# A fourth relation by Strassen's seven products, and key-row requests that wait one group further back, in a graph and feed-forward kernel

## Chip, cores and metric

The kernel runs on one core of one Trainium2 chip. The metric is the device time in microseconds (us) of one execution; for several executions their median is given.

## The reference, cut to what matters

Four layers follow one another on a node matrix x of 625 rows and 1024 columns, all float32. The change touches the first of them, a relational graph layer, and the list of edges that the third one uses too:

```python
xn = layernorm(x)
out = xn @ root + bias
for r in range(8):                                   # eight relations
    mask = (edge_type == r)
    sums = segment_sum(xn[src] * mask[:, None], dst, 625)
    mean = sums / maximum(segment_sum(mask, dst, 625), 1.0)[:, None]
    out = out + mean @ weight[r]                     # weight[r] is 1024 x 1024
```

There are 20,625 edges. After this come a gate, an 8-bit dense layer, a graph convolution over the same edges and a mixture of experts; the change leaves all of them as they are.

## The kernel before, in words

**Order of the mathematics.** The kernel computes h = xn @ weight[r] first for every relation (nine "units": relations 1 to 8, then unit 0, which is the root matrix), stores each h to memory, and then multiplies it by the relation's 625 x 625 matrix of edge counts ("spread"). `UNITS` gives the order 1, 2, ..., 8, 0; the index `n` in the loops is the place in that order.

**Products.** The 625 rows are five chunks of 125 (`C = 5`). A weight matrix is 16 tiles of 128 x 512: eight steps k over its rows, two halves `hf` of its columns. Every float32 number is kept as a high and a low part, and `three` (line 581) issues three matmuls for a chunk and a tile. `by_tile` (line 584) does one half of a unit: it takes five of the eight PSUM banks, one for each chunk, and runs 8 steps x 5 chunks x 3 = 120 matmuls, so a plain unit is 240. Five banks in turn out of eight mean that a new half finds three banks free; for its fourth and fifth chunk it waits until the first two chunks of the half before have been evicted. In unit 0 VectorE evicts; in plain units 1 to 8 ScalarE does, in `h_copy` (line 1104), one copy and one store for each of the five chunks, after it has done step k = 7 of that half.

**Units by Strassen's scheme.** The units in `FAST` (before: 6, 7, 8) go through `fast_unit` (line 637). The first four chunks are two 2 x 2 block problems, each done with seven block products instead of eight; the fifth chunk is computed plainly. That is 28 tiles (the seven `KINDS` times four), 72 products, 216 matmuls. Three of the seven weight blocks are loaded and used as they are; the other four are sums that VectorE makes in `fast_after` (line 1458, eight additions of 128 x 1024 by line 1418). VectorE also combines products (lines 1430, 1438, 1446), and ScalarE makes three copies of products (lines 1114, 1119) and three of the ten evictions; VectorE makes the other seven. The stationary sides, sums of blocks of xn, are made once, by `s_made` (VectorE, line 1496, 20 operations of line 1494 and 8 of line 1489) and `s_high` (ScalarE, line 1144, 8 casts), in the steps with odd k of the unit with n = `S_AT`: n = 3 (unit 4) before. ScalarE waits in `s_high` until VectorE has made the sum.

**The tile ring.** Weight tiles come over the SP queue (line 467) in groups of four into stages: two buffers in turn for plain units, and three further ones (C, D, E) for Strassen units. ScalarE makes the high part (line 403) and VectorE then the low part (line 412) in a ring of ten slots (`RT = 10`). At step k both do the tile nine places ahead; ScalarE can write a slot only when TensorE has used the tile ten places back.

**Key windows.** The counts of edges are built from a list of keys, one for each edge. VectorE compares 41 groups of four columns of keys with broadcast key rows (`key_window`, line 1564: four operations of line 1574, then two small ones, lines 1578 and 1581). `WINDOWS` says at which steps k of a plain half a window lies (before: 0, 2, 4, 6 of every half, from the second half of unit 1 on, with one window in the first half), and `KEYS_IN_FAST` at which tiles of a Strassen unit (before: 3, 10, 17, 24). By that the 41 windows are over within unit 6. The key rows lie in four buffers. ScalarE requests them by `key_rows` (line 1174), which first waits for the comparison that used the buffer four groups back; `next_key_rows` (line 1208) is called at the place of each window. At the place of window w, ScalarE's own counter g is w - 1, and before the change it requests group g + 5 = w + 4: it waits there for window w itself.

**From the windows to the spread.** GpSimd adds the counts of each group by four indirect DMAs (line 2215) into one of two scratch matrices. Up to group 9 all go to one of them, and each group waits until the group before has landed; from group 10 on they alternate. The scratch matrices are zeroed by DMAs, those of the second one on the SP queue, two with each of the weight groups 8 to 15. When the last group has landed and the last Strassen unit is evicted (`h_made` on VectorE, `if i - F0[u] == 37`), GpSimd fetches the matrices of relations 0 and 1 (lines 2243 and 2220), ScalarE copies them (`adjacency_copy`, line 1178), and TensorE begins to spread. The SP queue loads the h of each relation into the same two stages.

```python
            def key_rows(g):
                on.wait_ge(*at("equal", g - 4))
                e.dma_start(KR[:, g % 4, :], keyflat[...]...)
```

## Time and profile before

| what | value |
|---|---|
| median of 3 runs | 1142.88 us (1140.48 to 1143.81) |
| the profiled execution | 1138.64 us, of which the span is 1136.9 us |
| TensorE busy (matmul) | 1077.9 us, 95% of the span, 5433 matmuls |
| TensorE busy (weight load) | 902.2 us, 79% |
| VectorE busy | 751.3 us, 66% |
| ScalarE busy | 406.3 us, 36% |
| GpSimd busy | 400.9 us, 35% |
| mean granted TensorE clock | 0.976 of full speed |
| DMA | 217.34 MB, 191 GB/s over the span |

In the profile PE is TensorE (PEld its weight loads), DVE is VectorE, ACT ScalarE, POOL GpSimd, SP the queue of SyncE. A row names line, engine, operation, and the tiles written and read. The busy time of an engine is the union of its instructions. In a timeline each row begins with its start and its duration in us, and in brackets stands how long the engine was idle before it and who ended the wait. In a table by windows each engine has its busy time and the number of its instructions in that stretch; PEclk is the granted TensorE clock, where 1.00 is 2.4 GHz and 0.50 is 1.2 GHz. Matmuls overlap, so a matmul's own duration (0.40 us for 512 columns) is longer than the distance between two of them.

### The profile page before, as it was taken

Reading aid. Unit: us, or ns where it says so; the run is one execution under the profiler, and the core shown is the slowest. Engines: PE = TensorE matmul, PEld = TensorE weight load, DVE = VectorE, ACT = ScalarE, POOL = GpSimd, SP = SyncE. Lnnn points to the kernel's source line nnn. Section 1 sums busy time; section 2 is a strip of 40 time slices with the busy share of each in tenths; the row PEclk is TensorE's granted clock in tenths of the full one; section 3 lists DMA queues with packets and bytes.
Section 4 is the critical chain, followed back from the end, with each engine's and each line's share of the span. In section 5 each row is a group of like instructions: output and inputs, shape, how many; then the busy total and the mean of one; then the engine's idle time right before and its main releaser. Section 6 shows DMA issues by size and latency. Waiting matters only on the chain.

```text
span 1136.9 us, 14471 instructions
## 1 busy us (share of the span) xinstructions
PE 1077.9 (95%) x5433; PEld 902.2 (79%) x5433; DVE 751.3 (66%) x1529; ACT 406.3 (36%) x631; POOL 400.9 (35%) x272
## 2 busy tenths in 40 slices
PE   6979999897999999999999999799979999999996
PEld 5868888675888888888999999788856878878874
DVE  7466666767679785325666677466378738866657
ACT  3323222222243434312323333261433514337752
POOL 6044444688788888113322340000020000311016
PEclk9989999998999999999999999999989999989998
DMA  9988999777948465897999933442242011588757
GB/s 331 403 264 243 277 275 277 163 165 193 286 74 233 102 157 122 189 249 193 267 243 238 257 100 111 146 178 93 75 86 81 25 70 37 190 259 294 267 181 254
DMA packets 94474, 217.34 MB, mean 191 GB/s; under 512 B 29978, under 2 KB 46173, under 8 KB 85947
## 3 DMA queue, kind: packets, MB, share of 16 engines
q1 hardware_dynamic: 39488, 137.19, 36.6%
q0 software_dynamic: 37504, 48.18, 21.0%
q10 hardware_dynamic: 17406, 30.97, 9.3%
q8 instruction: 46, 0.75, 0.3%
q14 instruction: 30, 0.25, 0.1%
HBM read 149.59 MB, written 66.71 MB: 190 GB/s over the span
## 4 chain that ended last, share of the span: by engine, by line
PE 85%; DVE 10%; ACT 2%; issue 1%; DMA 1%; ACTq 0%; POOLq 0%; DVEq 0%; SPq 0%
PE ps L581 68%; PE ps L889 5%; PE ps L926 4%; DVE EQ L1574 3%; DVE rl L412 2%; PE ps L853 2%; PE ps L571 1%; ACT rh L403 1%; PE ps L904 1%; DVE V L1494 1%; PE ps L937 1%; PE ps L1020 1%; PE ps L806 1%; ACT He L1104 1%; PE ps L870 1%
## 5 line engine op out<-in xcount | busy, mean ns | idle before, releaser
L412 DVE TENSOR_TENSOR rl<-stage,rh 128x512 fp32r<-128x512 f32 (+1 forms) x276 | 222.7, 830 | 228.0 <-ACT rh L403 224.1
L403 ACT CAST rh<-stage 128x512 fp32r<-128x512 f32 (+1 forms) x276 | 188.5, 709 | 434.7 <-PE ps L581 237.6
L2215 POOL DMA_INDIRECT adj_scratch<-cnt,idx x164 | 271.4, 1655 | 157.6 <-issue 53.5
L581 PE MATMUL ps<-rh,xTh 128*125 128x512 f32 x680 | 271.5, 399 | 21.5 <-ACT He L1104 20.7
L581 PE MATMUL ps<-rl,xTh 128*125 128x512 f32 x680 | 269.3, 396 | 0.0
L581 PE MATMUL ps<-rh,xTl 128*125 128x512 f32 x680 | 269.1, 396 | 0.0
L581 PE MATMUL ps<-rh,Ar 125*125 125x342 f32 x600 | 190.1, 322 | 0.8 <-DVE U L1669 0.8
L581 PE MATMUL ps<-rl,Ar 125*125 125x342 f32 x600 | 189.5, 321 | 0.0
L581 PEld LDWEIGHTS ps<-rh,xTh 128*125 128x125 f32 x680 | 127.3, 187 | 54.8 <-ACT He L1104 22.1
L581 PEld LDWEIGHTS ps<-rh,xTl 128*125 128x125 f32 x680 | 127.4, 187 | 31.8
L581 PEld LDWEIGHTS ps<-rl,xTh 128*125 128x125 f32 x680 | 127.7, 188 | 30.7
L1574 DVE SCALAR_TENSOR_TENSOR EQ<-KR,kc,later 128x512 bf16<-128x512 f32 x164 | 113.4, 748 | 0.0
L581 PEld LDWEIGHTS ps<-rh,Ar 125*125 125x125 f32 x600 | 112.4, 187 | 1.1 <-issue 1.0
L581 PEld LDWEIGHTS ps<-rl,Ar 125*125 125x125 f32 x600 | 112.5, 188 | 0.0
L1669 DVE SCALAR_TENSOR_TENSOR U<-ps,rc,U 125x342 f32<-125x342 f32 (+1 forms) x120 | 66.2, 569 | 26.9 <-PE ps L581 24.6
L2233 POOL TENSOR_TENSOR Atot<-Atot,Ar 128x3125 f32<-128x3125 f32 x7 | 44.4, 6347 | 69.8 <-ACT Ar L1186 69.8
L581 PE MATMUL ps<-rh,uTh 128*125 128x512 f32 x160 | 63.5, 397 | 0.0
L2265 POOL DMA_DIRECT2D X<-in_fbias x6 | 6.0, 1118 | 162.2 <-ACT U L1157 162.2
L581 PE MATMUL ps<-rl,uTh 128*125 128x512 f32 x160 | 63.1, 394 | 0.0
L581 PE MATMUL ps<-rh,uTl 128*125 128x512 f32 x160 | 63.1, 394 | 0.0
L581 PE MATMUL ps<-rh,Sx 128*125 128x512 f32 x120 | 45.3, 394 | 0.0
L1104 ACT COPY He<-ps 125x512 f32<-125x512 f32 x59 | 34.1, 586 | 20.2 <-ACT He L1104 14.8
(295 smaller groups left out, 1494.0 us busy)
## 6 DMA issues: line engine op xcount, KB each, us to landing
stage<-in_w_rel SPq DMA_DIRECT2D x26, 1024.0 KB, 6.6
stage<-h_scratch SPq DMA_DIRECT2D x24, 855.0 KB, 7.1
stage<-in_w_e SPq DMA_DIRECT2D x16, 1024.0 KB, 5.2
adj_scratch<-Z POOLq DMA_DIRECT2D x16, 767.0 KB, 19.7
adj_scratch<-Z SPq DMA_DIRECT2D x16, 767.0 KB, 10.1
h_scratch<-He ACTq DMA_DIRECT2D x40, 257.0 KB, 9.2
h_scratch<-He ACTq DMA_DIRECT2D x40, 256.0 KB, 4.0
KR<-key_scratch ACTq DMA_DIRECT2D x37, 256.0 KB, 6.2
```

Of the source, the lines that this page charges most:

```text
L403: e.copy(h, s).then_inc(*a_hi.up(*[("hi", t) for t in step(i)]))
L412: e.tensor_tensor(l, s, h.bitcast(F32), ALU.subtract).then_inc(*v_lo.up(*[("lo", t) for t in step(i)]))
L571: ins = e.transpose(ps[:, b, j * P:(j + 1) * P], source[:, c, k * 128:(k + 1) * 128], ident[0:P, 0:P])
L581: ins = e.matmul(ps[0:P, b, 0:width], a, m, start=first and n == 0, stop=last and n == len(parts) - 1, skip_group_check=again)
L853: ins = e.matmul(ps[0:P, b, :], AT[:, k, c * P:(c + 1) * P], m[:, k, HALF[hf]], start=k == 0 and m is gh, stop=k == C - 1 and m is gl)
L889: ins = e.matmul(ps[:, b, 0:vn], a[:, ws], m[:, k, v0:v0 + vn], start=k == 0 and j == 0, stop=k == 7 and j == 2)
L926: ins = e.matmul(ps[0:HC, b, :], a, m, start=k == 0 and q == 0, stop=k == 1 and q == 2)
L1104: e.copy(He[0:P, n % NHE, 2:514], ps[0:P, b, :]).then_inc(*a_out.up(("he", u, c, hf)))
L1574: e.scalar_tensor_tensor(out=EQ[:, j, :], in0=KR[:, g % 4, :], scalar=kc[:, t:t + 1], in1=later[:, j0:j0 + TG * 128], op0=ALU.is_equal, op ...
L1669: e.scalar_tensor_tensor(out=U[:, c, to], in0=ps[0:P, b, cols], scalar=rc[:, r, c:c + 1], in1=U[:, c, to], op0=ALU.mult, op1=ALU.add).then ...
L2215: e.indirect_dma_start(accd[to], bass.IndirectOffsetOnAxis(ap=idx[:, n:n + 1], axis=0), cnt[:, n:n + 1], None, compute_op=ALU.add).then_in ...
L2233: e.tensor_tensor(flat, flat, arf, ALU.add).then_inc(*p_row.up(("total", r)))
```

## The change

Relation 5 becomes a Strassen unit as well (`FAST = (5, 6, 7, 8)`). The stationary sums move one unit earlier (`S_AT = 2`, unit 3). The 41 windows are laid out anew: five in unit 1 as before, eleven in unit 2, eight in unit 3, eleven in unit 4, six in unit 5, none after it. At the place of window w ScalarE now requests group g + 4 = w + 3, so that it waits for window w - 1. The third load of the root matrix goes into stage D, so the two common stages alternate the other way round from there on; ScalarE's copy of relation 1's matrix, which overwrites that stage, waits for the low parts of those four tiles. The last three evictions of the last Strassen unit lie one tile earlier on VectorE.

```diff
--- before.py
+++ after.py
@@ -39,7 +39,8 @@
 SW = 2048
 NHE = 8
 NB = 8
-WINDOWS = {(n, hf): (0, 2, 4, 6) for n in range(R + 1) for hf in range(2)}
+WINDOWS = {(0, 1): (0, 2, 4, 6), (1, 0): (0, 1, 2, 4, 5, 6), (1, 1): (0, 1, 3, 5, 6), (2, 0): (0, 2, 4, 6), (2, 1): (0, 2, 4, 6),
+           (3, 0): (0, 1, 2, 4, 5, 6), (3, 1): (0, 1, 3, 5, 6), (8, 0): (), (8, 1): ()}
 SOLE = 10
 ROWS = [[(slice(0, 128), c * P, 128)] for c in range(C - 1)] + [[(slice(0, 112), 500, 112), (slice(112, P), 612, 13)]]
 HALF = (slice(0, 512), slice(512, D))
@@ -47,11 +48,11 @@
 LATE = [(R - 2, 0), (R - 1, 0), (R - 2, 1), (R - 2, 2), (R - 1, 1), (R - 1, 2)]
 ORDER = [(r, q) for r in range(R - 2) for q in range(3)] + LATE
 UNITS = [*range(1, R + 1), 0]
-FAST = (6, 7, 8)
+FAST = (5, 6, 7, 8)
 KINDS = ("b11", "t2", "t3", "t1", "t4", "b21", "b22")
 FL = 4 * len(KINDS)
-KEYS_IN_FAST = (3, 10, 17, 24)
-S_AT = 3
+KEYS_IN_FAST = {5: (2, 7, 12, 17, 22, 26)}
+S_AT = 2
 
 
 class Count:
@@ -351,7 +352,8 @@
             else:
                 for q in range(4):
                     kind = ("root",) if u == 0 else ("rel", u - 1)
-                    group(w_root[q] if u == 0 else w_rel[4 * (u - 1) + q], 128, *[(*kind, q // 2, q % 2 * 4 + t) for t in range(4)])
+                    group(w_root[q] if u == 0 else w_rel[4 * (u - 1) + q], 128, *[(*kind, q // 2, q % 2 * 4 + t) for t in range(4)],
+                          where=3 if (u, q) == (0, 2) else None)
         h_of = lambda r: hd[r].rearrange("p (c w) -> p c w", c=C)
         for r, q in ORDER:
             group(h_of(r)[:, :, q * TH:(q + 1) * TH], P, *[("h", r, q, k) for k in range(C)], width=TH)
@@ -1180,6 +1182,9 @@
                 if r == 0:
                     on.wait_ge(*at("slot zero"))
                     on.wait_ge(*at("fast", FAST[-1], "b22", ("E", 2)))
+                if r == 1:
+                    for k in range(4):
+                        on.wait_ge(*at("lo", tile["root", 1, k]))
                 if r >= 2:
                     on.wait_ge(*at("spread", r - 2, 2, C - 1))
                     on.wait_ge(*at("total", r - 2))
@@ -1206,18 +1211,15 @@
             g = 0
 
             def next_key_rows(g):
-                if g < NG - 1:
-                    if g == 0:
-                        key_rows(4)
-                    if g + 5 < NG:
-                        key_rows(g + 5)
+                if g + 4 < NG:
+                    key_rows(g + 4)
                 return g + 1
 
             for n, unit in enumerate(UNITS):
                 if unit in FAST:
                     for l in range(FL):
                         highs(F0[unit] + l + RT)
-                        if l in KEYS_IN_FAST:
+                        if l in KEYS_IN_FAST.get(unit, ()):
                             g = next_key_rows(g)
                     continue
                 for hf in range(2):
@@ -1450,7 +1452,7 @@
                     if i - F0[u] == 29:
                         for p in range(2):
                             h_made(u, 2 * p + 1, 0, banks.of["fast", u, "Y", p], V2[0:P, p, :], ALU.add, ("fast", u, "t4", ("Y", p)), ("v2", u, p))
-                    if i - F0[u] == 37:
+                    if i - F0[u] == (36 if u == FAST[-1] else 37):
                         for p in range(2):
                             h_made(u, 2 * p, 1, banks.of["fast", u, "Z", p], V2[0:P, p, :], ALU.subtract, ("fast", u, "b22", ("Z", p)), ("v2", u, p))
                         h_made(u, 4, 1, banks.of["fast", u, "E", 2], V5[0:P, :], ALU.subtract, ("fast", u, "b22", ("E", 2)), ("v5", u))
@@ -1629,7 +1631,7 @@
                 if unit in FAST:
                     for l in range(FL):
                         lows(F0[unit] + l + RT)
-                        if l in KEYS_IN_FAST and g < NG:
+                        if l in KEYS_IN_FAST.get(unit, ()):
                             key_window(g)
                             g += 1
                     continue
```

## Rows read from the trace of the kernel before

**Rows 1.** Section 1 of the page: TensorE's busy time.

```profile
PE 1077.9 (95%) x5433; PEld 902.2 (79%) x5433; DVE 751.3 (66%) x1529; ACT 406.3 (36%) x631; POOL 400.9 (35%) x272
```

**Rows 2.** What TensorE waited for, 0 to 520 us: total, times, longest.

```profile
PE ps L581 <- ACT He L1104: 20.7, 3, 8.2
```

**Rows 3.** Table by windows: start and end, busy us and instructions of each engine.

```profile
50.00:100.00 50.00, 43.55 (x183) 34.62 (x182) 30.54 (x83) 10.91 (x19) 19.20 (x12) 0.93 0.81 255
150.00:200.00 50.00, 50.00 (x218) 40.19 (x217) 30.65 (x84) 13.97 (x24) 25.67 (x16) 1.00 1.00 288
200.00:250.00 50.00, 43.95 (x184) 34.94 (x183) 35.24 (x82) 13.35 (x23) 37.43 (x23) 0.93 0.72 165
250.00:300.00 50.00, 41.79 (x174) 33.11 (x174) 33.81 (x83) 14.11 (x25) 40.81 (x26) 0.93 0.83 210
```

**Rows 4.** Groups of instructions, 0 to 500 us: busy, mean ns, idle before.

```profile
L403 ACT CAST rh<-stage 128x512 fp32r<-128x512 f32 x132 | 78.6, 620 | 214.8 <-DVE idx L1581 127.5 <-PE ps L581 55.5 <-DMA stage<-in_w_rel 11.7
L412 DVE TENSOR_TENSOR rl<-stage,rh 128x512 fp32r<-128x512 f32 x132 | 88.2, 691 | 128.8 <-ACT rh L403 128.8
L1574 DVE SCALAR_TENSOR_TENSOR EQ<-KR,kc,later 128x512 bf16<-128x512 f32 x164 | 113.4, 748 | 0.0
L1418 DVE TENSOR_TENSOR stage<-stage,stageC 128x1024 f32<-128x1024 f32 x6 | 7.3, 1219 | 0.0
```

**Rows 5.** Timeline of TensorE: first matmul after each of the three waits.

```profile
81.88 0.79 PE L581 MATMUL ps<-rh,xTh 128*125 128x512 f32 x1 [6.45 <-ACT He L1104]
...
228.28 0.79 PE L581 MATMUL ps<-rh,xTh 128*125 128x512 f32 x1 [6.05 <-ACT He L1104]
...
266.11 0.79 PE L581 MATMUL ps<-rh,xTh 128*125 128x512 f32 x1 [8.21 <-ACT He L1104]
```

**Rows 6.** Timeline: one place in units two halves apart, and in two Strassen units.

```profile
135.04 0.58 ACT L1104 COPY He<-ps 125x512 f32<-125x512 f32 x1
...
190.50 0.58 ACT L1104 COPY He<-ps 125x512 f32<-125x512 f32 x1
...
398.40 0.68 DVE L1430 TENSOR_TENSOR He<-ps,V 125x512 f32<-125x512 f32 x1
...
448.49 0.68 DVE L1430 TENSOR_TENSOR He<-ps,V 125x512 f32<-125x512 f32 x1
```

**Rows 7.** Timeline of ScalarE and VectorE in unit 4, which makes the sums.

```profile
195.64 0.62 ACT L403 CAST rh<-stage 128x512 fp32r<-128x512 f32 x1 [0.40 <-ACT He L1104]
...
200.08 0.62 ACT L403 CAST rh<-stage 128x512 fp32r<-128x512 f32 x1 [3.82 <-DVE idx L1581]
...
200.73 0.69 DVE L412 TENSOR_TENSOR rl<-stage,rh 128x512 fp32r<-128x512 f32 x1 [0.66 <-ACT rh L403]
...
227.65 0.58 ACT L1104 COPY He<-ps 125x512 f32<-125x512 f32 x1
...
232.78 0.62 ACT L403 CAST rh<-stage 128x512 fp32r<-128x512 f32 x1 [0.40 <-ACT He L1104]
...
265.47 0.58 ACT L1104 COPY He<-ps 125x512 f32<-125x512 f32 x1
```

**Rows 8.** The indirect adds of GpSimd (line 2215), all 164: shape and landing.

```profile
L2215 POOL DMA_INDIRECT adj_scratch<-cnt,idx x164: 1531/1543/2568, 67.8 to 455.1; - x164
...
DMA to landing us min/median/max: 2.9/4.9/14.4
```

**Rows 9.** Timeline from the free-running adds to the first spread.

```profile
205.87 1.54 POOL L2215 DMA_INDIRECT adj_scratch<-cnt,idx  x1 [9.40 <-DMA adj_scratch<-cnt,idx]
...
455.09 1.54 POOL L2215 DMA_INDIRECT adj_scratch<-cnt,idx  x1 [0.30 <-issue]
...
476.32 0.95 POOL L2243 DMA_DIRECT2D AT<-adj_scratch  x1 [19.69 <-DVE rl L412]
...
511.29 2.81 ACT L1186 CAST Ar<-AT 128x3125 fp32r<-128x3125 f32 x1
...
526.80 0.32 PE L581 MATMUL ps<-rh,Ar 125*125 125x342 f32 x1
```

## The prediction

> **What bounds the kernel now.** The page first: TensorE is busy 95% of the span [rows 1], so a matmul less is time less, if nothing else takes its place. The view of waits for the first 520 us comes next: TensorE lost 20.7 us in three waits, all for ScalarE's evictions of products (line 1104), and next to nothing for weights [rows 2]. The table by windows prices them whole: an undisturbed stretch of 50 us has 218 matmuls, 0.2294 us each; the three stretches with a wait have 183, 184 and 174. That is 35, 34 and 44 matmuls short: 8.0, 7.8 and 10.1 us, 25.9 in all. It is more than the waits themselves (6.45, 6.05 and 8.21 us [rows 5]) because the granted clock is 0.93 in each of these stretches against 1.00 in the undisturbed one [rows 3]: after each wait TensorE restarts at the lower level, 1.2 GHz, and a restart costs some 1.8 us.
>
> Why is the eviction late? The view of groups says that ScalarE's casts of weights stood idle 127.5 us for VectorE's `idx`, the end of a key window, while VectorE's low parts stood idle 128.8 us for ScalarE's casts [rows 4]. The two engines run in lock-step: ScalarE stops at each request for key rows until the window of the same place is over. TensorE notices only where both are behind: at the end of unit 1, whose weights come late, and at the end of both halves of unit 4, where VectorE has the stationary sums too.
>
> **Part 1: a fourth relation.** Two evictions that lie two plain halves apart are 190.50 - 135.04 = 55.46 us apart; the same combination in two successive Strassen units is 448.49 - 398.40 = 50.09 us apart [rows 6]. 24 matmuls of 0.2294 us would be 5.5; I take the measured difference, **5.4 us** less.
>
> What it adds lies beside this: 12 more casts on ScalarE (0.62 each, 7.4 us), against seven evictions fewer and three copies more; on VectorE 12 more low parts (0.69, 8.3 us), eight sums (1.22, 9.8 us) and eleven combinations (0.68, 7.5 us) [rows 4, 6]. One window is four comparisons of 0.68 (113.4 us over 164, with their overlap) and two small ones, about 3.1 us. VectorE in unit 5 is then 28 low parts (19.3), sums (9.8), combinations (7.5) and six windows (18.6): 55.2 us against TensorE's 50.1, too much by 5.1 us (less where instructions overlap). The cover is the ring: VectorE works nine tiles ahead, at 50.1 / 28 = 1.8 us a tile some 16 us, and unit 6, with no windows, has 36.6 us of work in 50.1 and pays back. In unit 4's second half, where unit 5's eight sums are made already, it is eight low parts, eight sums and five windows: 5.5 + 9.8 + 15.5 = 30.8 against 27.7, late by 3.1 more. Together 8.2 us, half of the cover: nothing for TensorE. If the cover were gone, these 8 us would be the price.
>
> **Part 2: requests one group back.** ScalarE at window w waits for w - 1, one step or more past. Where windows lie two steps apart it was over long ago; where they lie at adjacent steps, one step of TensorE is 15 x 0.2294 = 3.44 us and VectorE needs 3.1 + 0.6, so ScalarE waits some tenths. The buffers get their rows three windows ahead instead of four: at least three steps, 10 us.
>
> *End of unit 1.* Without the stops ScalarE is at the eviction when TensorE has the product. Its last cast there needs weights whose load follows VectorE's low parts; VectorE was in those parts in time for TensorE, so I take the whole **8.0 us**; from below 0, if the load holds it.
>
> *The unit with the sums* (4 before, 3 after; with the same windows at the same steps, and 28 operations of VectorE and 8 casts in either place). Here ScalarE stays tied to VectorE: at each odd step it waits in `s_high` for the sum. So only part goes. The chain before: first eviction 190.50, first cast of the half 195.64, next first eviction 227.65, cast 232.78, eviction 265.47 [rows 6, 7]: evictions 5.1 us a half, work 32.0 and 32.7, or 37.2 and 37.8 where TensorE needs 27.7. The change takes from each window what VectorE loses when its low part has to wait for a cast held up by the request: 0.66 us [rows 7], some 0.7 with the gaps; four a half, 2.8 us. ScalarE also comes to the unit about 0.9 us sooner. First wait: 6.05 - 2.8 - 0.9 = 2.3 us. Second: the chain is 5.1 + 29.9 = 35.0 against 27.7, so 7.3 us and a restart of 1.8. Sum 11.4 in place of 7.8 + 10.1 = 17.9: **6.5 us** less. Bounds: 0 (ScalarE's order sets the pace all the same) and 17.9 (VectorE catches up). Between them the row of the 0.66 us is nearest.
>
> *Eleven windows in units 2 and 4.* Halves with six windows ask VectorE for 5.5 + 18.6 = 24.1 us, with five 21.0, in 27.7: fits.
>
> **Edits with one answer.** Root load in stage D and the wait for its four low parts, alternation of stages, one eviction group a tile earlier: no price. A root tile is split nine tiles before its use, and `adjacency_copy(1)`, behind which ScalarE's casts of h are queued, comes after all root tiles. The loads, stores, zero DMAs of SP and the 37 requests are the same in number; SP's stay tied to their group numbers. The latter have as cover the matmuls; if a load came late, I would see ScalarE wait for `stage`.
>
> **What is late next.** GpSimd's adds run without pause from 205.87 to 456.6 and don't depend on the windows any more by then; the fetch at 476.32 waited 19.69 us for VectorE's last evictions [rows 9]. With TensorE 19.9 us earlier that point is 456.4, and the fetch is set by the adds: 456.6 + 4.9 of landing [rows 8] = 461.5. From fetch to the end of ScalarE's copy it took 511.29 + 2.81 - 476.32 = 37.8 us, part of it waiting for its turn: 499.3. The first spread matmul, 526.80 before, is due at 506.9. So 7.6 us of cover are left of 12.7.
>
> **The sum.** 5.4 + 8.0 + 6.5 = 19.9 us. Against the profiled execution: 1138.6 - 19.9 = 1118.7. That execution lies 4.2 us below the median of the runs; against the median, 1142.9 - 19.9 = **1123.0 us**.
>
> **The rivals.**
> *A. As above*, 1123; its own range 1118 to 1128. Chance 0.55.
> *B. All three waits go.* For it: VectorE has 34 to 35 us of work in the 50 of the two stretches [rows 3], so it isn't full, and ScalarE is freed of 127.5 us of idling. Against it: `s_high` still ties them. 1142.9 - 5.4 - 25.9 = 1111.6. Chance 0.14.
> *C. VectorE takes over as the bound* where windows are packed, above all in units 4 and 5: its 8.2 us are not covered because it comes late out of the unit with the sums. 1123.0 + 8.2 = 1131.2, about 1127 if half shows. Chance 0.17.
> *D. The request's wait doesn't go*, since window w - 1 is unfinished too (at adjacent steps it is so by tenths, by the figures above): only 5.4 stays, 1137.5. Chance 0.05.
> *E. GpSimd is held up by VectorE.* An add took 1.54 us at the median but up to 2.57 [rows 8], and from 205.87 to 455.09 the 123 distances average 2.03 us against 1.84 (1.54 and the 0.30 of issue) [rows 9]: 23 us lost, in a stretch where VectorE's operations mostly read two tensors in SBUF. The change puts 20 more such operations into unit 5. If the loss doubled, the adds would end at 479.6, the matrix be ready at 479.6 + 4.9 + 37.8 = 522.3, and TensorE wait 15.4 us: 1138.4. Chance 0.05: 20 operations more don't double it. The Trainium skill ("SBUF — State Buffer", section "SBUF: two separate sides") speaks against the change in this way: VectorE with two SBUF inputs and GpSimd share a port pair as an exclusive lock, and a DMA whose descriptors GpSimd makes can starve behind it. By that rule E, by the median row A; the trace agrees with it only as far as the 2.57 goes.
> *F. Slower than before: the first ten groups of adds.* They run one after another, each waiting for the landing of the last, 67.8 to 205.87 [rows 8, 9], 13.8 us a group, at a DMA share of 1.00 [rows 3]. The change packs more requests and the zero DMAs of SP into that stretch. It decides once the fetch passes 506.9 - 37.8 = 469.1; to be 0.3% slower than before, the spread must begin after 530.2, the fetch after 492.4, which is 31 us past 461.5, or 3.1 us more for each of the ten groups. 3.5 us each give 1147. Against it: 37 requests stay 37, and the longest landing of any add is 14.4 us. Chance 0.04.
>
> **How the numbers follow.** A measurement of this kernel can tell about 0.3%, 3.4 us, from no change. A, B, C, D, E are faster by more than that: 0.96, less 0.02 for what D and E hold near the edge; F is slower, 0.04; within 0.3% 0.02. The range reaches from B, 1111, to C, 1131: it leaves out D, E and F (0.14) and a little at the ends.
>
> **What would show it.** Right: a Strassen unit of 50.1 us as the fifth unit; no wait near 75 us; ScalarE's idling for `idx` from 127.5 to under 20 us; TensorE's waits for evictions near 10 us in two, in unit 3 (about 160 and 195 us); the fetch of line 2243 released by an add and not by VectorE; the first spread near 507. Wrong: no wait at all in unit 3 (B), a wait of TensorE for `rl` in units 4 to 6 (C), ScalarE idle for `idx` as before (D), TensorE idle before the first spread (E, F).

## The result, and the profile after

| | before | after |
|---|---|---|
| median of 4 runs | 1142.82 us (1140.48 to 1143.81) | 1157.99 us (1157.09 to 1160.41) |
| the profiled execution; its span | 1138.64 us; 1136.9 us | 1158.23 us; 1156.5 us |
| mean granted TensorE clock | 0.976 | 0.965 |

The kernel became slower: ratio 1.0148, 95% interval 1.0123 to 1.0172. The forecast was 1123.0 us, with a range from 1111 to 1131 us.

The code has moved by two lines (581 is now 583, 412 is 414). The first section of the page after the change, to set beside [rows 1]:

```profile
PE 1077.9 (93%) x5409; PEld 900.9 (78%) x5409; DVE 777.8 (67%) x1560; ACT 411.8 (36%) x639; POOL 407.1 (35%) x272
```

24 matmuls fewer are there, but the busy time is the same: some of it was run at the lower clock. Section 2, 40 slices of 28.9 us each, shows where:

```profile
PE   6999998999999999953999999899978999999995
...
PEclk9999999999999999986899999999998999989997
```

TensorE's 18th and 19th slices (491 to 549 us) stand at 5 and 3, and the clock falls to 8, 6 and 8 from the 18th to the 20th. What TensorE waited for after the change, whole span, the four largest:

```profile
PE ps L583 <- issue: 25.7, 1, 25.7
PE ps L573 <- DVE U L1548: 9.2, 1, 9.2
PE ps L583 <- DVE rl L414: 8.9, 1, 8.9
PE ps L583 <- ACT He L1106: 7.0, 2, 4.9
```

The last row answers to [rows 2]: 20.7 us in three waits became 7.0 in two. The first and third are new. (`rl` is the low part of a tile, `Ar` a relation's matrix, `He` the evicted product.) TensorE's timeline says where each one ends (the 9.2 us of line 573 lies at the very start of the kernel, where it was 9.6 us before the change):

```profile
161.01 0.49 PE L583 MATMUL ps<-rh,xTh 128*125 128x512 f32 x1 [2.08 <-ACT He L1106]
...
195.71 0.58 PE L583 MATMUL ps<-rh,xTh 128*125 128x512 f32 x1 [4.87 <-ACT He L1106]
...
532.53 0.62 PE L583 MATMUL ps<-rh,Ar 125*125 125x342 f32 x1 [25.74 <-issue]
...
551.64 0.65 PE L583 MATMUL ps<-rh,Ar 125*125 125x342 f32 x1 [8.87 <-DVE rl L414]
```

**The account.** The row at 532.53 is the first spread matmul. TensorE was free for it at 532.53 - 25.74 = 506.79 us. Before the change it began at 526.80 [rows 9], without a wait. So up to there the change had saved **20.0 us**, and the forecast had said 19.9. Then it gave back 25.7 and 8.9. The span grew by 19.6, so 19.6 + 20.0 - 25.7 - 8.9 = 5.0 us remain. No row shows them one by one, but the table by windows shows the lower clock level around both waits:

```profile
500.00:550.00 50.00, 17.03 (x80) 15.09 (x78) 10.55 (x6) 8.74 (x4) 15.01 (x7) 0.70 0.78 191
510.00:532.00 22.00, 0.00 (x0) 0.00 (x0) 0.00 (x0) 2.36 (x1) 4.97 (x4) 0.50 0.95 247
552.00:560.00 8.00, 8.00 (x36) 8.00 (x36) 7.05 (x17) 0.00 (x0) 0.00 (x0) 0.64 0.93 275
```

In an idle stretch the granted clock is 0.50 (1.2 GHz), and just after the second wait it is still 0.64. After that nothing differs: from ScalarE's copy of relation 2's matrix (552.29 us before, 572.05 after, 19.8 later) both kernels need the same time to the end.

**Why was the matrix late?** "issue" names nobody. The chain is read backwards from 532.53 in the timelines of ScalarE and GpSimd:

```profile
529.64 2.80 ACT L1191 CAST Ar<-AT 128x3125 fp32r<-128x3125 f32 x1 [38.41 <-DMA AT<-adj_scratch]
```

```profile
70.10 1.69 POOL L2217 DMA_INDIRECT adj_scratch<-cnt,idx  x1 [42.79 <-DVE idx L1583]
...
242.09 1.54 POOL L2217 DMA_INDIRECT adj_scratch<-cnt,idx  x1 [14.38 <-DVE EQ L1576]
...
493.14 1.54 POOL L2217 DMA_INDIRECT adj_scratch<-cnt,idx  x1 [0.30 <-issue]
...
510.37 0.95 POOL L2245 DMA_DIRECT2D AT<-adj_scratch  x1 [15.68 <-issue]
```

The copy that TensorE needs is ready at 532.44, the fetch for it went out at 510.37, the last add at 493.14, and the first of the free-running adds (group 10) at 242.09 instead of 205.87 [rows 9]. That is 36.2 us later, and the last add is 38.1 us later (455.09 before): the delay of the adds arises almost wholly *ahead of group 10*. From there to the matrix two pieces follow: 15.7 us from the end of the last add (494.68) to the fetch, and 22.1 us from the fetch to the end of ScalarE's copy. The ten groups in front of it took (242.09 - 70.10) / 10 = 17.2 us each instead of 13.8. The window of group 10 isn't what they wait for: VectorE made it at 103 us in the changed kernel, at 122 before. From each group's four rows: issuing them took 7.95 us on average (7.31 before), and then GpSimd stood 9.25 us (6.49 before) until they had landed. From group 10 on a group takes 8.18 us, against 8.11.

### The profile page after: what moved, and what is told of

Read it like the earlier page. It is cut to its first block, busy times and chain, and to the rows that moved or that the text cites. A ratio compares the mean times of both kernels' runs of the same rounds, so it can differ in the third digit from the quotient of the medians.

```text
span 1156.5 us, 14474 instructions
## 1 busy us (share of the span) xinstructions
PE 1077.9 (93%) x5409; PEld 900.9 (78%) x5409; DVE 777.8 (67%) x1560; ACT 411.8 (36%) x639; POOL 407.1 (35%) x272
## 4 chain that ended last, share of the span: by engine, by line
PE 86%; DVE 7%; issue 3%; DMA 2%; ACT 1%; POOLq 0%; ACTq 0%; DVEq 0%; SPq 0%
PE ps L583 69%; PE ps L891 5%; PE ps L928 4%; DVE rl L414 2%; PE ps L855 2%; PE ps L573 1%; PE ps L906 1%; DVE EQ L1576 1%; DMA stage<-in_w_rel 1%; PE ps L939 1%; ACT rh L405 1%; PE ps L808 1%; PE ps L872 1%; DVE st L1525 1%; DVE X L2063 1%
## 5 line engine op out<-in xcount | busy, mean ns | idle before, releaser
L2217 POOL DMA_INDIRECT adj_scratch<-cnt,idx x164 | 277.6, 1692 | 189.8 <-DVE idx L1583 60.4
L405 ACT CAST rh<-stage 128x512 fp32r<-128x512 f32 (+1 forms) x268 | 183.5, 712 | 363.9 <-PE ps L583 244.2
L583 PE MATMUL ps<-rh,xTh 128*125 128x512 f32 x640 | 255.1, 399 | 7.5 <-ACT He L1106 7.0
L583 PE MATMUL ps<-rl,xTh 128*125 128x512 f32 x640 | 253.2, 396 | 0.0
L583 PE MATMUL ps<-rh,xTl 128*125 128x512 f32 x640 | 253.0, 395 | 0.0
L583 PE MATMUL ps<-rh,Ar 125*125 125x342 f32 x600 | 193.9, 328 | 35.4 <-issue 25.7
L583 PEld LDWEIGHTS ps<-rh,xTh 128*125 128x125 f32 x640 | 119.5, 187 | 39.6 <-ACT He L1106 9.7
L583 PEld LDWEIGHTS ps<-rh,xTl 128*125 128x125 f32 x640 | 119.6, 187 | 30.2
L583 PEld LDWEIGHTS ps<-rl,xTh 128*125 128x125 f32 x640 | 119.6, 187 | 29.1
L583 PE MATMUL ps<-rh,Sx 128*125 128x512 f32 x160 | 60.4, 394 | 0.0
L583 PE MATMUL ps<-rl,Sx 128*125 128x512 f32 x128 | 50.5, 395 | 0.0
```

The costliest lines, as they stand in the source:

```text
L405: e.copy(h, s).then_inc(*a_hi.up(*[("hi", t) for t in step(i)]))
L583: ins = e.matmul(ps[0:P, b, 0:width], a, m, start=first and n == 0, stop=last and n == len(parts) - 1, skip_group_check=again)
L2217: e.indirect_dma_start(accd[to], bass.IndirectOffsetOnAxis(ap=idx[:, n:n + 1], axis=0), cnt[:, n:n + 1], None, compute_op=ALU.add).then_in ...
```

## The experiments

Theory 1, after the result: **the serial groups.** Traffic in the DMA queues in 70 to 240 us makes each landing longer, so the adds end 38 us later. Rivals: VectorE's denser work holds up GpSimd's own descriptor work (rival E, in another place); or the new place of the requests does it by itself. In all runs below "group 10" is the start of its first add, and "the gap" is GpSimd's mean idle time from the end of one group's issue to the next group's start, for the groups 0 to 9. Each is read from one trace. Up to group 8 the changed kernel and four of the kernels below run the same program, and there group 8 starts at 203.9, 204.4, 199.3, 208.1 and 206.2 us: 9 us between them with no edit that could act there.

### Part 2 alone, and part 2 undone

The kernel before, with the new request distance only:

```diff
-                    if g + 5 < NG:
-                        key_rows(g + 5)
+                if g + 4 < NG:
+                    key_rows(g + 4)
```

> The kernel before with one part of the change alone: at the place of window w ScalarE requests group w + 3 and so waits for window w - 1. Three relations by Strassen's scheme, windows and sums as before. Theory 1 (the eleven windows in unit 2 crowd the first ten groups of adds, which run one after another): here the windows stay spread, group 10 starts near 206 to 212 us as before, the adds end by 462, and the time is 1142.8 - 14.5 = 1128 us. Theory 2 (requests that are free of VectorE crowd them, whatever the windows): group 10 starts at 230 us or later, the adds end past 480, and the time is 1143 us or more.

Measured: 1125.46 us against 1139.15 on the same chip, ratio 0.9885 (0.9868 to 0.9903), 13.7 us less. TensorE's waits, up to the end of the products, and the adds:

```profile
PE ps L581 <- ACT He L1104: 7.5, 2, 5.0
```

```profile
208.78 2.04 POOL L2212 DMA_INDIRECT adj_scratch<-cnt,idx  x1 [2.83 <-DMA adj_scratch<-cnt,idx]
...
459.55 1.54 POOL L2212 DMA_INDIRECT adj_scratch<-cnt,idx  x1 [0.30 <-issue]
```

The requests alone bring nearly the whole gain of part 2 and move group 10 by 2.9 us only. They are not the cause by themselves.

The changed kernel with the old distance (the same diff, reversed):

> The changed kernel with the old requests: at the place of window w ScalarE requests group w + 4 and waits for window w. Everything else as changed (four relations, eleven windows in unit 2). Theory 1 (window layout): group 10 starts well after 206 us, at 225 or later, because the windows and their requests are as dense; TensorE waits before the first spread, and adds to that its old waits for evictions at the end of unit 1 and in unit 3: 1158 us or more. Theory 2 (free requests): group 10 starts near 210, no wait before the first spread; 5.4 us of the relation are left, about 1137 us.

Measured: 1157.26 us, ratio 1.0161 (1.0141 to 1.0181): no different from the changed kernel, and yet group 10 starts at 197.85, 44 us earlier, and the adds end at 472.6. The time is lost elsewhere:

```profile
PE ps L583 <- ACT He L1106: 30.8, 6, 8.6
PE ps L583 <- DVE V L1443: 5.0, 1, 5.0
```

Theory 1 had group 10 wrong here. With the windows this dense, the old requests stop ScalarE so often that TensorE waits six times (the fetch, at 494.85, is then released by VectorE and not by an add). TensorE's waits hold back the weights too: in 70 to 200 us the DMA engines move 218 GB/s here and 261 in the changed kernel, and the gap is 5.50 us. That the slower traffic makes the landings quick fits the pair of experiments below but isn't isolated here. The zero writes come later as well: group 11 waits 20.0 us for them, and starts at 225.3 where the kernel before had 213.4:

```profile
225.26 1.54 POOL L2220 DMA_INDIRECT adj_scratch<-cnt,idx  x1 [20.02 <-DMA adj_scratch<-Z]
```

So neither part alone gives the late group 10: not the free requests (208.78), nor the dense windows (197.85).

### Dense windows

The changed kernel with windows at steps 0, 2, 4, 6 of each half in units 1 to 4 and six each in units 5 and 6:

```diff
-WINDOWS = {(0, 1): (0, 2, 4, 6), (1, 0): (0, 1, 2, 4, 5, 6), ...}
+WINDOWS = {(n, hf): (0, 2, 4, 6) for n in range(4) for hf in range(2)} | {(8, 0): (), (8, 1): ()}
-KEYS_IN_FAST = {5: (2, 7, 12, 17, 22, 26)}
+KEYS_IN_FAST = {5: (2, 7, 12, 17, 22, 26), 6: (2, 7, 12, 17, 22, 26)}
```

> The changed kernel with eight windows instead of eleven in units 2 and 4, and six in unit 6 that were in these: the densest stretch is thinned. Theory 1 (window layout): group 10 starts by 215 us, adds end by 468, the fetch is then near 475 and the wait before the first spread shrinks from 26 to about 6 us or less: 1130 us or below. Theory 2 (free requests, or VectorE holding GpSimd up at any density): group 10 still starts past 230 us, 1150 us or more.

Measured: 1133.84 us, ratio 0.9957 (0.994 to 0.9973). Group 10 at 215.67, end of the adds 473.6: 26 and 21 us earlier than in the changed kernel, a little short of the expectation, and the time missed it by 4 us. The wait with "issue" is gone though the fetch went out only at 481.54, but another has grown:

```profile
PE ps L582 <- DVE rl L413: 12.4, 2, 12.1
```

That is the second wait of the changed kernel, and longer; it is taken up below.

### What the gain is without the wait

The changed kernel without the last eight of the 41 groups of adds, so that their edge counts are left out; the fetch waits for the last two groups that remain:

```diff
-            for g in range(NG):
+            for g in range(NG - 8):
                 to = adder(g)
...
-                on.wait_ge(*at("added", NG - 2))
-                on.wait_ge(*at("added", NG - 1))
+                on.wait_ge(*at("added", NG - 10))
+                on.wait_ge(*at("added", NG - 9))
```

> The changed kernel without the last 8 of the 41 groups of indirect adds (so the edge counts of these are left out); nothing else. The adds then end near 430 us instead of 495. If the late end of the adds is all that made the change slower, both waits of TensorE after the root unit (25.7 and 8.9 us) and their restarts are gone, and the time is the predicted one, 1143 - 20 = 1123 us. If the wait has another cause (the h of relation 0, the fetch itself), TensorE still waits over 15 us before the first spread and the time stays above 1145 us.

Measured: 1118.95 us against 1139.15, ratio 0.9824 (0.9807 to 0.9842), **20.2 us less**. Group 10 is as late as before (241.0), but the adds end at 432.3, and no wait stands before the spread. The fetch is released by the last evictions:

```profile
453.38 0.95 POOL L2245 DMA_DIRECT2D AT<-adj_scratch  x1 [21.05 <-DVE rl L414]
```

So the end of the adds is what cost the time, the two waits hang on it, and behind it lies the forecast gain.

### Traffic or VectorE?

Theory 1 and the rival about VectorE part where traffic alone changes. Two kernels do that, in either direction. In the first, SP's sixteen zero writes go out with the weight groups 14 to 21 instead of 8 to 15, and `SOLE` (the group from which adds alternate) is 20 so that they are there in time; groups 0 to 9 go to the first matrix either way:

```diff
-SOLE = 10
+SOLE = 20
...
-                if 8 <= g < 16:
+                if 14 <= g < 22:
```

> The changed kernel with the SP queue's sixteen zero writes of the second scratch matrix moved from the weight groups 8 to 15 to the groups 14 to 21, and SOLE = 20, so that groups 0 to 19 all go to the first matrix. Only the start times of groups 1 to 9 are wanted (the time gets worse, since twice as many groups wait for a landing). Theory 1a (the zero writes lengthen the landings): the mean gap between these groups falls from 9.3 us to 6 us or less. Theory 1b (the key rows and the weights do it): it stays at 8 us or more.

In the second, the kernel of the first experiment requests each key row of groups 4 to 24 twice, the second time into a stage that is free:

```diff
                     key_rows(g + 4)
+                    if g + 4 <= 24:
+                        extra_rows(g + 4)
```

> The kernel of the first experiment (requests one group back alone) in which each request for groups 4 to 24 is sent twice, the second time into a stage that isn't used yet. Theory 1b (key-row requests in the DMA queues lengthen the landing of an add): the mean gap between groups 0 to 10 rises from 6.4 us to 8.5 or more, and group 10 starts past 225 us instead of 209. Theory 2 (VectorE's work does it): VectorE does the same as before, so group 10 stays within 205 to 214 us.

The table by windows for 70 to 200 us, first the kernel before, then the changed kernel, the one with late zero writes, requests alone, and requests doubled:

```profile
70.00:200.00 130.00, 123.56 (x529) 98.91 (x528) 83.41 (x232) 37.04 (x63) 62.13 (x39) 0.97 0.94 262
```

```profile
70.00:200.00 130.00, 122.87 (x514) 96.65 (x513) 103.70 (x275) 39.06 (x68) 56.04 (x32) 0.97 0.92 261
```

```profile
70.00:200.00 130.00, 121.65 (x517) 96.31 (x516) 104.42 (x279) 38.91 (x67) 69.37 (x40) 0.98 0.72 185
```

```profile
70.00:200.00 130.00, 129.95 (x562) 103.77 (x561) 87.80 (x244) 39.03 (x65) 60.77 (x36) 1.00 0.98 269
```

```profile
70.00:200.00 130.00, 129.78 (x560) 103.41 (x559) 87.92 (x244) 39.11 (x65) 45.30 (x27) 1.00 1.04 309
```

VectorE (the third pair of numbers) is the same within a pair of kernels, 103.70 and 104.42, 87.80 and 87.92. What differs is the DMA share in the last columns and GpSimd's own count of instructions: 32 and 40, 36 and 27. And so the adds:

| kernel | GB/s | issue of a group | gap | group 10 |
|---|---|---|---|---|
| before | 262 | 7.31 | 6.49 | 205.87 |
| dense windows, old requests | 218 | 7.50 | 5.50 | 197.85 |
| changed | 261 | 7.95 | 9.25 | 242.09 |
| zero writes late | 185 | 7.95 | 5.90 | 207.50 |
| requests alone | 269 | 7.78 | 6.39 | 208.78 |
| requests doubled | 309 | 7.76 | 9.64 | 241.32 |

The traffic moves group 10 by 34.6 us down or 32.5 us up, with VectorE's work unchanged, well beyond the 9 us between traces of the same program. So traffic alone can make the whole delay (requests doubled, VectorE at 87.9), and VectorE's dense work without the zero writes doesn't make it (104.4, gap 5.90). As an explanation by itself the rival falls.

What changed between the kernel before and the changed one isn't the amount of traffic, though: 262 and 261 GB/s, and on the two hardware queues 22.67 and 11.24 MB before against 22.70 and 11.05 after, all in 70 to 200 us. Its place in time did change: 196 GB/s became 252 in 70 to 100 us, 268 became 220 in 160 to 190. So which transfers stand just ahead of an add probably counts, and how the key rows and zero writes of the changed kernel meet was not taken apart. Nor is it excluded that VectorE's denser work (83.4 to 103.7 us) adds something together with that traffic: no run changes it alone. The 0.64 us of longer issue (7.31 to 7.95) stays when the zero writes go, and 7.78 is there with the requests alone: that part is something else, and open.

The kernel with late zero writes took 1178.27 us (one run; 41.2 us of waiting before the spread; groups 10 to 19 were serial as well and the adds ended at 523.3), the one with doubled requests 1151.39 us (one run, 14.6 us of waiting before the spread).

### Alternating earlier

> The changed kernel with SOLE = 8: the adds alternate between the two scratch matrices from group 8 on instead of 10, so two landings fewer are waited for (7.7 and 14.4 us in the changed kernel). Theory 1 (the serial groups set the end of the adds, and that sets the spread): the adds end near 474 us instead of 495, the wait before the first spread falls from 26 us to about 5 to 8, and the time falls by about 20 us. Theory 2 (GpSimd's work as a whole, or VectorE holding it up, sets the end): the adds end after 487 us and at most 7 us are gained.

`SOLE = 8` instead of 10 and nothing else: 1139.27 us (ten runs, 1132.3 to 1143.83), ratio 0.9981 (0.9956 to 1.0006). Group 10 starts at 216.42 and the adds end at 472.2, as expected, 22.5 us earlier; the time fell by 18.7 us against the changed kernel's median (taken on another chip), not to the level of the experiment without the last adds, because the second wait was there again (before the first spread there was none, with the fetch at 479.70):

```profile
PE ps L583 <- DVE rl L414: 12.4, 2, 12.1
```

### The second wait

After the first spread matmul, ScalarE had to copy relation 1's matrix before it could cast the next block of h, and VectorE then made its low part. The timelines of the changed kernel:

```profile
538.55 2.81 ACT L1191 CAST Ar<-acb 128x3125 fp32r<-128x3125 f32 x1 [6.12 <-DMA acb<-adj_scratch]
541.26 3.25 ACT L405 CAST rh<-stage 125x1710 fp32r<-125x1710 f32 x2
...
542.90 8.68 DVE L414 TENSOR_TENSOR rl<-stage,rh 125x1710 fp32r<-125x1710 f32 x1 [35.38 <-ACT rh L405]
543.45 6.34 POOL L2235 TENSOR_TENSOR Atot<-Atot,Ar 128x3125 f32<-128x3125 f32 x1
```

A low part of this size takes 1.94 us where no addition of GpSimd runs beside it; here 8.68. GpSimd's addition ends at 549.79 and the low part at 551.58, 1.8 us behind it, as if it had begun only then. Two edits tell the parts apart. One shortens GpSimd's addition of relation 1 to 25 of its 3125 columns (the total then lacks the rest of that relation), the other moves ScalarE's copy of that matrix behind the cast of the second third of relation 0's h:

```diff
-                    e.tensor_tensor(flat, flat, arf, ALU.add)...
+                    n = 25 if r == 1 else C * N
+                    e.tensor_tensor(flat[:, 0:n], flat[:, 0:n], arf[:, 0:n], ALU.add)...
```

> The changed kernel, in which GpSimd's addition of relation 1's matrix to the total covers 25 columns instead of 3125 (so the degrees are left incomplete). In the changed kernel the low part of the second third of h took 8.68 us on VectorE beside that addition of 6.34 us, and 1.9 to 2.0 us elsewhere. Theory L (the two engines lock each other out): here it takes about 2 us and TensorE's second wait falls from 8.9 us to 2 to 3 us. Theory N (something else, such as the late cast, makes it long): it stays above 6 us, the wait above 6 us.

```profile
535.93 1.94 DVE L414 TENSOR_TENSOR rl<-stage,rh 125x1710 fp32r<-125x1710 f32 x1 [28.13 <-ACT rh L405]
```

The low part is back at 1.94 us, and the waits for `rl` fall from 8.9 us to 3.3 in two. That GpSimd's addition held it is shown. The Trainium skill ("SBUF — State Buffer", section "SBUF: two separate sides") says that a VectorE operation with two SBUF inputs and a GpSimd operation that reads SBUF share a port pair as an exclusive lock; the 8.68 and 1.94 agree with that. It also says that whichever starts first gets the pair for its whole instruction. There the trace doesn't agree as it stands: VectorE's row begins at 542.90, 0.55 us ahead of GpSimd's, and yet VectorE is the one that was held. The run took 1143.68 us (one run; 18.5 us of waiting for the matrix remained; its adds ended at 493.1 and its fetch came 7.8 us later, at 500.92, 9.5 us earlier than in the changed kernel, which explains most of the rest).

```diff
-            adjacency_copy(1)
             for r, q in ORDER[:-2]:
                 highs(tile["h", r, q, 0] + RT)
+                if (r, q) == (0, 0):
+                    adjacency_copy(1)
```

> The changed kernel with SOLE = 8 and ScalarE's copy of relation 1's matrix behind the cast of the second third of relation 0's h. With SOLE = 8 alone (ratio 0.998 to the kernel before) TensorE still waited 12.1 us for a low part after the first five spread chunks. Theory: that second wait is the order on ScalarE (the copy waits for its fetch, the cast is queued behind it); with the copy moved it is gone, 12 to 16 us less than with SOLE = 8 alone: ratio 0.984 to 0.988. If it's the fetch of h or VectorE alone, the wait stays over 8 us and the ratio above 0.993.

With `SOLE = 8` and this: 1137.71 us (ten runs, 1127.26 to 1143.77), ratio 0.9955 (0.9926 to 0.9984). The expectation missed. The wait for `rl` shrank to 4.5 us in three, but one of 12.3 us for the first matrix was back: group 10 at 225.58, 9 us later than without the moved copy, which lies at 500 us and can't act on it; and the fetch came 15.9 us after the adds, where the other kernels whose adds set the fetch have 6.7 to 10.0, all but the changed one with 15.7. The first must come from something that varies from run to run, and the 16.5 us between its ten runs fit that; for the second it is only likely. What varies is not known.

### Versions that keep the gain

The thin windows, `SOLE = 8` and the moved copy together:

> A version that might beat both: the changed kernel with at most eight windows in a plain unit (six in unit 6), SOLE = 8, and ScalarE's copy of relation 1's matrix behind the cast of the second third of relation 0's h instead of ahead of it. Theory 1: the adds end by about 462 us, the first spread comes without a wait, the second wait (12.1 us for the low part in the thinned version) goes with the copy's new place: 20 us faster than the kernel before, like the version without the last adds. Theory 2: adds end past 470 us all the same, a wait of 8 us or more stays, and it is 12 us faster at most.

Measured: **1121.9 us** (four runs, 1120.19 to 1124.04), ratio 0.9842 (0.9815 to 0.9868). GpSimd's adds, and the only wait of TensorE for an eviction or a weight before the spread:

```profile
210.19 1.54 POOL L2217 DMA_INDIRECT adj_scratch<-cnt,idx  x1 [0.30 <-issue]
...
465.13 1.54 POOL L2217 DMA_INDIRECT adj_scratch<-cnt,idx  x1 [0.30 <-issue]
```

```profile
PE ps L582 <- ACT He L1105: 8.3, 2, 6.2
```

Next, the 8.3 us: only two windows in each half of the unit with the sums, the four others in unit 7.

```diff
+WINDOWS = {(n, hf): (0, 4) if n == 2 else (0, 2, 4, 6) for n in range(4) for hf in range(2)} | {(8, 0): (), (8, 1): ()}
...
+KEYS_IN_FAST = {5: (2, 7, 12, 17, 22, 26), 6: (2, 7, 12, 17, 22, 26), 7: (3, 10, 17, 24)}
```

> The version of the eighth experiment (eight windows at most, SOLE = 8, the copy moved) with only two windows instead of four in each half of the unit that makes the sums, and those four windows in unit 7. Theory (my chain of the sums unit: casts, window, low part, sum in lock-step): each half gets 6.2 us shorter, to about 29 us with the evictions against TensorE's 27.7, so both waits for evictions (2.1 and 6.2 us) and the restarts after them go: 8 to 10 us less than the eighth, ratio to the kernel before 0.974 to 0.978. Rival: the evictions or something else sets the pace there; the waits stay over 4 us and the gain under 3 us.

Both waits for `He` went (0.2 us is left), which confirms the chain of that unit (28 operations for the sums, the evictions, the windows). The time didn't follow, and the expectation missed: 1130.1 us, the median of eight runs from 1123.72 to 1140.75, ratio 0.9874 (0.9849 to 0.9899) without the longest of them, with 9.9 us of "issue" and 5.3 us of `rl` before and in the spread, since the adds ended at 474.7. It looks like the same exchange as in the change itself, on a smaller scale: TensorE was free for the spread at 496.6, some 12 us earlier than in the version before, and the fetch went out 8.6 us later.

Last, that kernel with SP's zero writes two weight groups earlier and `SOLE = 6`:

> The version of the eleventh experiment with the sixteen zero writes of the second scratch matrix at the weight groups 6 to 13 instead of 8 to 15, and SOLE = 6, so that the adds alternate from group 6 on. Theory 1 (once the sums unit has no waits, the serial groups set the time): the zero writes have landed near 175 us, the adds free-run from about there and end by 460 us instead of 475; the wait of 9.9 us before the first spread goes, ratio to the kernel before 0.970 to 0.977. Rival: the zero writes, now earlier, lengthen the first landings as much as is saved, or weights come late on TensorE's side; the adds end past 468 us and the ratio stays above 0.982.

Group 10 at 201.36, adds ended at 462.2, no wait before the spread and 5.8 us of `rl` in it: 1123.19 us, the median of eight runs from 1110.21 to 1132.58. That is 0.983 of the 1142.6 us of the kernel before on the same chip; the four shortest of the eight alone, 1110.21 to 1119.25, give 0.972 (0.9695 to 0.9746). These are the shortest times of all the versions, but by its median and its spread this version isn't better than the one with 1121.9 us.

## Why the prediction was wrong, point by point

- **What bounds the kernel, part 1, part 2: right.** The gain up to the spread was 20.0 us, forecast 19.9; without the late adds the whole kernel gained 20.2. Requests alone gave 13.7 (forecast 8.0 + 6.5 = 14.5), so 6.5 us are left for the fourth relation (forecast 5.4). A place in unit 5 and the same in unit 6 are 328.15 - 278.22 = 49.9 us apart, forecast 50.1. The waits in unit 3 were 2.1 and 4.9 us; I had 2.3 and 7.3. The wait near 75 us was gone. Of the table by windows, three rows that answer to [rows 3]:

```profile
50.00:100.00 50.00, 49.91 (x215) 39.45 (x214) 37.67 (x109) 12.78 (x23) 14.14 (x8) 1.00 0.96 293
150.00:200.00 50.00, 42.96 (x171) 33.21 (x170) 36.19 (x85) 14.64 (x26) 21.26 (x12) 0.93 0.81 222
200.00:250.00 50.00, 50.00 (x218) 40.09 (x217) 46.03 (x121) 12.16 (x21) 21.32 (x12) 1.00 0.87 247
```

- **ScalarE's idling for `idx`: partly.** It fell from 127.5 to 49.0 us, not under 20: windows at adjacent steps do hold the request (without them it is 9.3 us with requests alone and 9.2 with thin windows). It hit no eviction that TensorE missed beyond those forecast.

```profile
L405 ACT CAST rh<-stage 128x512 fp32r<-128x512 f32 (+1 forms) x125 | 75.5, 629 | 160.2 <-PE ps L583 80.9 <-DVE idx L1583 49.0 <-DMA stage<-in_w_rel 11.7
```

- **"What is late next": this step failed.** It said that the adds "run without pause from 205.87 to 456.6 and don't depend on the windows any more by then", and so took both numbers over into the changed kernel. The second half of the sentence is true, the adds went on at 8.18 us a group. But 205.87 is itself the end of ten serial landings, in the very stretch into which the change packs eleven windows in unit 2 where eight were. They took 3.4 us more each and the end moved to 494.7. What was wrong first of all was the moment at which the resource it compares came free. TensorE's free time (506.9, measured 506.8) was right.
- **The 7.6 us of cover: too small, and wrong in two terms that nearly cancel.** The 37.8 us from fetch to copy isn't what the matrix needs. In the kernel before, ScalarE's copy stood behind a cast of h that waited for TensorE, and so moves with TensorE:

```profile
509.76 1.63 ACT L403 CAST rh<-stage 125x1710 fp32r<-125x1710 f32 x1 [16.82 <-PE ps L581]
```

  Where ScalarE did wait for the matrix, it took 22.1 us in the changed kernel and 21.4 to 26.6 in the other runs; with 22.1 the forecast's cover would have been 506.9 - 483.6 = 23.3 us. And the step from the last add to the fetch, put at the median landing of 4.9 us, took 15.7 us in the changed kernel and 6.7 to 10.0 in most others. With the end of the adds at 494.7 the forecast's terms would give 537.4 for the matrix; it came at 532.4.
- **The second joint was not in the sum.** Relation 1's matrix has to be copied before the next block of h is cast. In the two kernels with the fetch near 480 (thin windows, `SOLE = 8`) that cost 12.1 us, where the first spread waited for nothing.
- **Rival F was the outcome, at 0.04.** Place and mechanism were right: ten serial landings that lengthen. The decision point, a fetch after 469.1, was not, since it rests on the 37.8: fetches at 479.70 and 481.54 left the first spread without a wait. Nor was the size needed for a loss of 0.3%, 3.1 us a group. That 3.4 came and the loss was there is partly luck: a fetch 15.7 us behind the adds and the second wait made up for what the 37.8 had too much. Two things spoke for it in my rows and were set aside: each of these groups waits for a landing, at a DMA share of 1.00 [rows 3]; and landings spread from 2.9 to 14.4 us [rows 8]. "37 requests stay 37" holds, for the traffic of the stretch as a whole too (262 and 261 GB/s), and says nothing of where it lies. A small cause in each link of a chain of ten is a large one.
- **F's own price was too low, and by a slip.** 3.5 us a group make 461.5 + 35 + 37.8 = 534.3, 7.5 us past the 526.80 of before: 1150, not the 1147 that stands there. For the 3.4 us measured it is 1149.4. The 8.6 us between that and the 1158.0 measured come from the second wait (8.9 us) and the time at the lower clock (5.0 us), neither of which was in the sum, less the 4.2 us by which the profiled execution of before lies below its median and the 0.8 us by which the spread began sooner than these terms give.
- **Rivals B, C, D.** B fell, two waits stayed in unit 3. C fell, no wait for `rl` came in units 4 to 6. D fell by the 13.7 us of requests alone.
- **Rival E.** Not in its own place: free-running adds took 8.18 us a group against 8.11. But the two engines do lock each other out, the other way about and later: GpSimd's addition held VectorE's low part for 6.7 us. In the kernel before the same pair met for less: 4.16 us in place of 1.94.

## What to carry to other kernels

When a change makes the main engine earlier, list each resource that must be ready at the joint, and follow each one back to the start of *its* chain; a time read from the old trace may be carried over only if nothing of that chain lies in the stretch that is being repacked. A duration read from the old trace needs the same care: ask whether it was work or waiting for a turn. A chain of small dependent transfers is priced per link: here 3.4 us in each of ten links, with the second wait behind them, outweighed a saving of 20 us. And a stall may be protecting something: the waits for key rows set the pace of the requests and of the weights, so after removing one, look at what the traffic it held back now meets.

## What was not expected of the hardware

- The same four indirect adds leave GpSimd waiting 5.9 us or 9.6 us for their landing (means over ten gaps), depending on other DMAs in flight, and not by their mean GB/s alone. Requesting key rows a second time, 21 transfers in all, was enough for 3.3 us in each gap.
- A VectorE subtraction of 125 x 1710 takes 1.94 us alone and 8.68 us when it starts beside a GpSimd addition of 6.34 us. It ends 1.8 us behind GpSimd's, though its row begins 0.55 us ahead of it. The 1.8 us are there in the kernel before too, where it started 4.0 us into an addition of 6.35:

```profile
528.73 4.16 DVE L412 TENSOR_TENSOR rl<-stage,rh 125x1710 fp32r<-125x1710 f32 x1 [1.04 <-ACT rh L403]
```

```profile
524.74 6.35 POOL L2233 TENSOR_TENSOR Atot<-Atot,Ar 128x3125 f32<-128x3125 f32 x1
```

- Open: why the fetch followed the last add by 15.7 us in the changed kernel and 15.9 in one other, and by 6.7 to 10.0 in the rest; the longer issue of a group; which transfers lengthen the landings in the changed kernel; and why kernels with `SOLE` of 6 or 8 spread over 11 to 22 us from run to run, when the thin one with the moved copy kept within 3.9 us in its four.
